# First layer's side work given new points among the heads, and unread identity products on TensorE in long waits

## The reference, cut to what matters

```
x = x + 0.5 * ffn0(layernorm(x))      # base product, top 2 of 8 low-rank experts
x = x + attn0(layernorm(x))           # 16 heads of 16, q k v o each with a low-rank update
x = x + 0.5 * ffn0(layernorm(x))
x = x + 0.5 * moe1(layernorm(x))      # top 4 of 32 experts, silu gate, 2048 tokens
x = x + attn1(layernorm(x))           # latent attention, 16 heads, causal
x = x + 0.5 * moe1(layernorm(x))
```

## Time and profile before

| | us |
|---|---|
| runs before, median of 3 (lowest, highest) | 1552.89 (1550.59, 1554.79) |
| the profiled execution | 1556.93 |
| its span, first to last instruction | 1555.1 |
| mean granted TensorE clock | 0.889 |
| PE busy in the span | 1224.5 (79%) |
| DVE busy | 935.5 (60%) |
| ACT, POOL busy | 676.1, 547.7 |

### The profile page before, as it was taken

One profiled execution on the slowest core, in us unless ns is written; L12 is line 12 of the kernel. 1 busy time (PEld: TensorE's weight loads), 2 busy tenths in 40 slices (PEclk: granted clock), 3 DMA queues, 4 the chain that ended last, 5 costly groups with the idle time before them and its releaser, 6 DMA issues.

```text
span 1555.1 us, 20966 instructions
## 1 busy us (share of the span) xinstructions
PE 1224.5 (79%) x5960; PEld 751.6 (48%) x5960; DVE 935.5 (60%) x2702; ACT 676.1 (43%) x1706; POOL 547.7 (35%) x558
## 2 busy tenths in 40 slices
PE   4777877887878528999556989889989999299990
PEld 2432333332232316888423546555655656188870
DVE  6777566856754312232359887988788695232227
ACT  2223544554647114555324554455355354155550
POOL 2053270246353134555121121144125133455550
PEclk8786897998989759999779999999999999699995
DMA  4657065092031345554301000020001001444448
GB/s 117 109 93 205 21 88 177 21 164 101 26 138 39 125 165 190 164 160 149 133 13 42 28 28 1 1 79 31 1 11 45 33 33 44 149 160 156 156 136 274
DMA packets 80379, 147.94 MB, mean 95 GB/s; under 512 B 13885, under 2 KB 62078, under 8 KB 77326
## 3 DMA queue, kind: packets, MB, share of 16 engines
q1 hardware_dynamic: 62286, 104.41, 24.0%
q0 software_dynamic: 17408, 42.00, 7.6%
q10 hardware_dynamic: 576, 0.18, 0.0%
HBM read 83.21 MB, written 63.00 MB: 94 GB/s over the span
## 4 chain that ended last, share of the span: by engine, by line
PE 53%; DVE 28%; issue 7%; ACT 6%; DMA 2%; POOL 2%; SPq 1%; another core or an unknown queue 1%; DVEq 0%; POOLq 0%; ACTq 0%
PE m_psG L1057 11%; PE m_psY L1073 5%; DVE a_t L1483 4%; PE a_psO L414 3%; DVE a_mx L758 3%; PE a_psA L1251 3%; PE a_psU L389 3%; DVE a_nb L1491 3%; PE a_psS L400 3%; PE m_psX L1048 3%; PE a_psU L1233 2%; PE a_psT L310 2%; PE a_psU L1239 2%; PE a_psO L1274 2%; ACT a_pr L1354 2%
## 5 line engine op out<-in xcount | busy, mean ns | idle before, releaser
L138 POOL DMA_INDIRECT outs_dram<-m_ys,dest x192 | 184.0, 958 | 165.7 <-ACT m_ys L996 152.8
L1354 ACT ACTIVATE a_pr<-a_psA,a_nb 128x512 f32<-128x512 f32 (+3 forms) x256 | 132.6, 524 | 220.4 <-DVE a_nb L1491 219.5
L758 DVE TENSOR_REDUCE a_mx<-a_psU 128x1 f32<-128x512 f32 x256 | 165.2, 684 | 104.8 <-PE a_psU L389 91.0
L1016 DVE TENSOR_TENSOR m_hm<-m_psG,m_sg 128x128 f32<-128x128 f32 x192 | 55.9, 291 | 282.7 <-ACT m_sg L990 173.6
L1410 POOL TENSOR_TENSOR a_q<-a_q,a_t 64x512 f32<-64x512 f32 x64 | 80.8, 1263 | 358.0 <-DVEq L1486 336.2
L1057 PE MATMUL m_psG<-arena,m_xgT 128*128 x768 | 205.6, 391 | 0.8 <-issue 0.2
L533 ACT ACTIVATE a_P<-a_psS 128x512 f32<-128x512 f32 x256 | 143.6, 597 | 93.6 <-PE a_psS L400 80.2
L138 POOL DMA_INDIRECT rows_dram<-a_xd,slot x128 | 124.7, 974 | 142.5 <-DVE a_xd L124 76.2
L389 PE MATMUL a_psU<-arena 96*128 96x512 bf16 x256 | 108.0, 428 | 45.8 <-DVE a_mx L758 35.3
L1057 PEld LDWEIGHTS m_psG<-arena,m_xgT 128*128 128x128 f32 x768 | 133.5, 194 | 16.1 <-issue 4.0
L1491 DVE TENSOR_REDUCE a_nb<-a_psA 128x1 f32<-128x512 f32 (+3 forms) x256 | 113.2, 484 | 36.8 <-PE a_psA L1253 27.1
(11 more groups left out here) (249 smaller groups left out, 2222.7 us busy)
## 6 DMA issues: line engine op xcount, KB each, us to landing
m_xg<-rows_dram SPq DMA_DIRECT2D x48, 512.0 KB
arena<-in_mo_w SPq DMA_DIRECT2D x9, 2048.0 KB
arena<-part_dram SPq DMA_DIRECT2D x96, 128.0 KB
rows_dram<-arena SPq DMA_DIRECT2D x12, 1024.0 KB, 12.1
arena<-outs_dram SPq DMA_DIRECT2D x16, 512.0 KB, 3.6
part_dram<-a_part SPq DMA_DIRECT2D x16, 384.0 KB
m_xg<-outs_dram SPq DMA_DIRECT2D x8, 512.0 KB, 4.4
m_ys<-outs_dram SPq DMA_DIRECT2D x8, 512.0 KB, 5.0
```

Of the source, the lines that this page charges most:

```text
L138: pool.indirect_dma_start(out=rows_dram, out_offset=bass.IndirectOffsetOnAxis(ap=slot[:, c:c + 1], axis=0), in_=row, in_offset=None).then_ ...
L758: dve.tensor_reduce(mx[g % 2][:, 4 * kt + qt:4 * kt + qt + 1], psU[n % 2][:, :], AX, ALU.max).then_inc(u_free, 1)
L1354: ins = act.activation(pr[S % 2][:, AT[t]:AT[t] + (t + 1) * P], psA[:, AT[t]:AT[t] + (t + 1) * P], ACT.Exp, bias=nb[S % 2][:, t:t + 1], sc ...
```

## The change

**New points.** The chains begin elsewhere: F1 moves from 7 to 20, F2 from 25 to 33 (so to point 1 of the next i, with b = i - 2). Their parts are spread: main products one to a point instead of two and one and one, the gates cut in two, the transposes of the gated rows three points after. `batch_scales` is cut into `scales_begin` and `scales_end` with four points between for the attention's rows and one or two for the others. The products of q, k and v move from points 7 to 10 to points 15 to 18, while their rows are made at 13. `bases` and `places` move by a few points.

**POOL's order.** `route` is done in one piece right after the first `bias`, ahead of the terms of batch 1; the scattered writes of an i are no longer interleaved by thirds but stand in one run each, 22 or 21 of `entry` ahead of the terms, 16 of `rows` behind them.

**The zeros.** Half of `rows_dram` is filled at the very start from a part of `Pr` that POOL sets to zero first, the other half at i = 0. The six transfers at i = 1 are gone.

**Identity products.** `stay_warm(pe, bank, ident, n)` issues n products of the 128 x 128 fp32 identity with itself into a bank that nobody reads at the time. There are 201: 14 + 10 + 10 at the start of the first layer, 3 + 3 + 16 + 9 in its last chain, 26 at the start of each expert stage (behind a new semaphore `stored`, raised by POOL when it has issued the last row), and 40, 3, 3, 3, 24, 8, 3 in the latent stage's opening.

```diff
-    F1, F2 = 7, 25
-    QSC, QLN, QT, QK, QV = 0, 1, 2, 3, 7
-    AT, OP, OA, OST, OSC = 19, 20, 21, 23, 24
+    F1, F2 = 20, 33
+    TX, GM, GAP, GA, GB, TH, LM, LA, ST, SB, SE, XD = 1, (2, 3, 4, 5), 6, 7, 8, 9, 10, 11, {1: 12, 2: 13}, 14, 16, 18
+    QSC, QLN, QT, QK, QV = (7, 11), 13, 14, 15, 17
+    AT, OP, OA, OST, OSC = 19, 20, 21, 23, (29, 30)
...
-        for n, at, b in ((1, F1, i + 2), (2, F2, i - 1), (2, F2 - PTS, i - 2)):
+        for n, at, b in ((1, F1, i + 2), (1, F1 - PTS, i + 1), (2, F2 - PTS, i - 2)):
...
+def scales_end(dve, link, sc):
+    root_steps(dve, link, sc.var[:, :], sc.rstd[:, :], sc.tmp[:, :], 2)
...
+def stay_warm(pe, bank, ident, n):
+    for _ in range(n):
+        pe.matmul(bank[:, 0:P], ident[:, :], ident[:, :], start=True, stop=True, skip_group_check=True)
...
+            IDLE = {("q", 0, 0): 10, ("h", 1, 1): 10}
+            IDLE_LAST = {("ao", B - 1, 0): 3, ("ao", B - 1, 1): 3, ("x", 2, B - 1, 0): 16, ("h", 2, B - 1): 9}
...
+            stay_warm(pe, psO, ident, 14)
...
+            pool.memset(blank, 0.0).then_inc(blanked, 1)
...
-            for i in range(-2, B + 2):
+            for i in range(0, B + 2):
                 b = i + 1
-                if 1 <= b < B:
+                if i == 0:
+                    pool.wait_ge(rest_in, 16 * NREST)
+                if i < B:
+                    bias(i)
+                if i == 0:
+                    for part_of in range(3):
+                        route(part_of)
+                if 1 <= i <= 3:
+                    entry((0, 22, 43)[i - 1], (22, 43, 64)[i - 1])
+                if b < B:
                     for c in range(4):
                         terms(b, c)
-                for q, lo, hi in ((0, 0, 4), (1, 4, 10), (2, 10, 16)):
...
+                if 0 <= i - 2 < B:
+                    rows(i - 2, 0, TPB * TOPK)
...
+            sp.wait_ge(blanked, 1)
+            clear(0, blank)
...
+            pe.wait_ge(stored, 1)
+            stay_warm(pe, psY[1], ident, 26)
...
             for key in opening[:-2]:
-                if key == ("k", 0, 0):
+                if key == ("x", 0, 0):
+                    pe.wait_ge(added, 2 * TOPK)
+                    stay_warm(pe, psO, ident, 40)
+                elif key == ("qT", 0, 0):
+                    stay_warm(pe, psO, ident, 24)
+                elif key == ("k", 0, 0):
+                    stay_warm(pe, psO, ident, 8)
                     pe.wait_ge(kn_ready, 1)
+                else:
+                    stay_warm(pe, psO, ident, 3)
```

More of the change, by code:

```diff
@@ L183, in turn_units @@
         out = []
[L184 to L187, removed]
+        if ffn_at(i, p, TX):
+            out += [("x",) + ffn_at(i, p, TX) + (u,) for u in range(2)]
+        if ffn_at(i, p, TH):
+            out.append(("h",) + ffn_at(i, p, TH))
         if p == QT and 0 <= i + 1 < B:
@@ L200, in main_units @@
         out = []
-        for step, js in ((2, (0, 1)), (3, (2,)), (4, (3,))):
+        for j, step in enumerate(GM):
             if ffn_at(i, p, step):
-                out += [("m",) + ffn_at(i, p, step) + (j,) for j in js]
-        if ffn_at(i, p, 8):
-            out += [("l",) + ffn_at(i, p, 8) + (c,) for c in range(2)]
+                out.append(("m",) + ffn_at(i, p, step) + (j,))
+        if ffn_at(i, p, LM):
+            out += [("l",) + ffn_at(i, p, LM) + (c,) for c in range(2)]
         if QK <= p < QK + 4 and 0 <= i + 1 < B:
@@ L738, in side @@
                 if 0 <= b < B:
-                    if p in (OA, OA + 1):
+                    if p == OA:
                         dve.wait_ge(biased, TPB * (b + 1))
-                        add(("p", b, p - OA), b, p - OA)
+                        for u in range(2):
+                            add(("p", b, u), b, u)
                     if p == OST:
@@ L815, in rows @@
                 if b == 0 and lo == 0:
-                    pool.wait_ge(rows_clear, 16 * 12)
+                    for n in range(2):
+                        pool.wait_ge(wiped[n], 16 * 6)
                 for n in range(lo, hi):
@@ L853, in _, with clear @@
                              ).then_inc(pads_in, 16)
-            def clear(lo, hi):
-                w = zero.shape[1]
+            def clear(half, source):
+                w = source.shape[1]
                 rows = rows_dram.rearrange("(p j) d -> p (j d)", p=P)
-                for n in range(lo, hi):
-                    sp.dma_start(rows[:, n * w:(n + 1) * w], zero).then_inc(rows_clear, 16)
+                for n in range(6 * half, 6 * half + 6):
+                    sp.dma_start(rows[:, n * w:(n + 1) * w], source).then_inc(wiped[half], 16)
+            sp.wait_ge(blanked, 1)
+            clear(0, blank)
             for i in range(-2, B + 2):
@@ L1417, in _ @@
             store(B - 1, 0, TPB * TOPK)
+            pool.sem_inc(stored, 1)
             for n in range(2):
@@ L1691, in program @@
                     (bv[:, :], a["at_bias_v"]), (bo[:, :], a["at_bias_o"]), (weight[:, :], a["mo_weight"])])
-        moe = lambda tag, placed, loads, latent, result: moe_stage(
-            nc, block, sem, tag, r, ident, arena[:, :], (experts_in, 16 * loads), slot, weight, block_expert, rows_dram, placed,
+        moe = lambda tag, placed, stored, loads, latent, result: moe_stage(
+            nc, block, sem, tag, r, ident, arena[:, :], (experts_in, 16 * loads), slot, weight, block_expert, rows_dram, placed, stored,
             outs_dram, dest, dest_in, latent, result)
```

132 lines of the change are left out of this document (73 added, 59 removed).

## The result

The changed kernel took 1584.03 us (median, 1581.30 to 1587.44), the kernel before 1553.14 beside it: a ratio of 1.0201, 95% interval 1.0173 to 1.0230. It is slower, where 1500 us and a gain were predicted.

What follows compares the result with a forecast made beforehand. The prediction held that PE, DVE and ACT waiting for each other bound the first layer's heads, and half clock the serial stretches. 1556.9 - 42 - 11 = 1504, 4.0 above the median, so 1500 us; range 1472 to 1538.

Steps and rivals of the forecast that it cites:

- The step that failed: First layer's heads: POOL's runs of 22 scattered writes delay later terms by at most 5 us; taken as 0.
- Term 1: First layer's heads: spreading the side work over new points gives -42 us, ends -62 and -14.
- DVE's wait for PE: In the heads, DVE's wait for PE's blocks should fall from 72 us to under 45.
- The table sums: POOL's sums, moved to the start of batch 0, should stall DVE less: worth a few us of 88.7.
- The late terms: POOL's terms for the next batch, behind the scattered writes: lateness bounded by 5 us in batch 1, taken as 0.
- Term 2: Identity products keep PE's clock up in serial stretches: -6 - 4 - 3 + 2 = -11 us.
- the start: Identity products at the start: 8 us to win, DVE on most of that path, so -3; ends -8 and +2.
- the opening: Latent stage's opening: identity products hold the clock at 1.00, -6 us; ends -9 and +9.
- The starts of the expert stages: Identity products after the last row's issue run partly cold: +1 us for each of two stages, +2 together.
- the four: Lumps only move, 1528, 0.24; clock follows, 1478, 0.12; products outlast their waits, 1575, 0.05; nothing to be seen, 1553, 0.04.
- Rival 3: Latent opening and expert stage starts: identity products outlast their waits, +36 us, 1575 in whole; chance 0.05.
- slower: Whole kernel slower than before by more than 0.3% (5 us): chance 0.05.

Runs made afterwards that it cites:

- third call: Group of kernels measured together: the unedited changed kernel took 1490.95 us (0.9769) beside the kernel before at 1529.02; no late signals of PE.
- the fours: Changed kernel with a landing wait after every fourth scattered write, entries and rows, and terms moved ahead: 1503.95 us (0.9837) and 1502.31 us (0.9686).
- first: Group of kernels measured together, kernel before at 1532.58 us; the changed kernel without identity products took 1506.51 us (0.9824) there.
- e1: Changed kernel with POOL's order of before (thirds, each waited for, terms ahead): 1493.03 us, 0.9752; run again later: 1517.78 us, 0.9772.
- the pauses: Changed kernel with four small POOL fills after every fourth entry, rows in runs of 16: 1509.29 us (0.9871) and 1546.67 us (0.9957).
- e2: Kernel before with POOL's new order alone (long runs, entries ahead of terms): 1543.88 us, 1.0075; run again later: 1622.42 us, 1.0450.

## Why the prediction failed

**The step that failed** is "POOL's scattered writes come in runs of 22 ... I take 0 and keep 5 for the range". I asked only whether the run would make POOL's next job late, not what it does to the engines beside it. Where the stalls occur, this step costs 454.6 - 377.4 = 77 us in the heads (changed kernel, first trace against third call) and 8 more behind them: from the heads' end to the last scattered row 69.8 us for 61.4. There a run of 16 rows stands beside the last chain, and one DVE step waited 14.71 us for PE. These 85 are most of the 90 us between the two traces; 2.9 lie ahead of the heads and the rest behind.

That the kernel took 1490.95 us in the third call, near the 1500 predicted, is in part luck: the sum took 42 and 11 us from a before of 1553, and in that call before took 1529.02.

The Trainium skill, SBUF — State Buffer, section "SBUF: two separate sides", holds that of the engines only DVE and GpSimd share a port and that TensorE never waits on anyone there. The windows above show that TensorE's signals do come late beside GpSimd's scattered writes in some calls (33 products in 22.5 us for 98). No run shows that an SBUF port is the path, so this doesn't contradict the page.

**Term 1**, -42, gave the right heads but not the right gain. Where nothing stalls, the heads took 377.4 us for the forecast 387, the batches 87.8, 92.0 and 81.0 for 91, 91 and 78.5. With the fours they take 382.0 in a call with stalls too, against 429.2, 425.9 and 424.9 of before, 43 to 47 us less. But part of what I read in the earlier trace rows as the price of thick side work was stall already: before varies from 417.5 to 429.2 us, and at about 1530 us in whole it would be shorter still, by some 20 us if all of the difference lies in the heads (an estimate, for no trace of it is from such a call). So where nothing stalls the changed kernel gains 38.1 us and not 53, and without the products, which is term 1 alone, 22.6 us (third call) or 26.1 (first) and not 42. This is the second step that was mis-sized.

**DVE's wait for PE**, forecast under 45, is 46.9 in the quiet call, 56.6 in the first trace. **The table sums** won nothing: point 8 of batch 0 is 6.6 us with them at the new place and 2.8 without; point 25 is 3.2 and 7.5 (changed against e1); the batch is about as long either way (85.6 and 84.8). **The late terms** were 0 with the new points, as taken; the pauses show what they can cost (18.7 us at point 18), and `e2` that with the old points they came.

**Term 2**, -11: without the products the kernel takes 1506.41 for 1490.95 in the third call, 15.5 us more, and the call with stalls 10.2 more than the 1580.36 of another call. By the profiles of the third call it is 12.0 in all: 3.8 at the start (3 forecast), 1.6 in the heads, 1.7 from there to the first expert stage (4 forecast), 4.5 from the start of that stage to the start of the second (6 forecast for the opening), 0.4 behind. So the sum was about right, with parts that were off both ways. The starts of the expert stages cost 0, not +2, because their products came too early to do either harm or good. That step was wrong in mechanism: a signal behind a scattered write is not a signal that the write is issued.

**Rivals.** None of the four named it. Rival 3 had the right sign and the wrong cause, and the 0.05 on "slower" carried too much confidence that every stall was known.

**The best version** depends on the call: the changed kernel or its twin with the old order (1490.95, 1493.03) where nothing stalls, the fours everywhere (1502.31) where it does. The fours took less than the kernel before in both (0.9837, 0.9686), and so did the old order (0.9752, 0.9772).

## What to carry to other kernels

When an engine's transfers are regrouped, ask what the longer run does to the engines beside it, not only who waits for its end; look in the trace of before for idle time that the view gives to "remote" on one core. In this kernel a pause after every fourth scattered write (with the terms moved ahead) cost 13.0 us where nothing stalls; where it does, the kernel took 1502 us with it in one call and 1580 without it in another. And before explaining a result, run the unedited kernel again another time: here the same two programs compare as 1.020 and as 0.977.

## What the runs showed of the hardware

- In some calls a run of GpSimd's scattered writes at 1.26 us each makes TensorE's signals late: 14 to 19 of the 256 for the maxima came over 2 us after the product's start, up to 13.2 us, where 0.40 us is the median, and all of them in such a run or within about 1 us of its end. In the first trace the first such wait of DVE begins 10.7 us into the run, after 8 writes, and lasts 5.0 us, the next begins at 19.2 and lasts 9.8. Fours with 1.5 us between them showed none. With runs of 4 to 8 there were 2 to 8 late signals, up to 6.6 us. In other calls runs of 22 showed none.
- What makes such a call stays open. It is not the chip alone, if the number 11 of the third and fifth calls names one device. By which path TensorE's signals are held stays open too, and so does whether recording has a part in it. Few bytes were moving (DMA share 0.02 in the window).
- The clock falls with it: 0.61 in the window for 1.00, so the products behind a stall are slow as well (one of 512 columns is drawn 0.61 us long at 189.16, 0.39 in the fours).
- POOL's queue sends a signal placed behind scattered writes 11.4 us before the last of them begins (585.84 against 597.25).
